# A decoder layer on one core: the last router scores and the second search move over the loop's edge, and the written order is renewed

## The reference

```
x = x + attention(norm(x))           # 16 heads of 32 columns, softmax over 224 keys, output product Wff
x = x + cross_attention(ctx, norm(x))# one head of 512 columns, softmax over 750 keys
x = x + ffn(norm(x)):
    query  = h @ q_proj.T ; rq = query @ router_w.T        # 48 columns
    scores = rq @ (aux_keys @ router_w.T).T / sqrt(48) + mask   # 224 x 2048
    top_scores, top_idx = top_k(scores, 8)
    agg  = sum over 8 of softmax(top_scores) * aux_values[top_idx]
    gate = sigmoid(w * clip(0.5 * log variance part + 2.5 * sigmoid(learned part)) + b)
    out  = h + gate * agg
```

## Time and profile before

| What | Value |
|---|---|
| median of the runs | 2769.6 us |
| the profiled execution: its time, its span | 2767.93 us, 2766.1 us |
| busy: PE, PEld, DVE, ACT, POOL | 2549.4, 2107.2, 1976.6, 1442.4, 862.9 us |
| PE busy between 400 and 2500 us | 2049.95 of 2100 us, granted clock 1.00 |
| one iteration, from A `score` 0 to the next | 79.1 us |
| DVE, ACT, POOL busy in one iteration | 60.9, 43.4, 26.0 us |
| PE busy between 2600 and 2700 us, and after 2700 us | 56.95 us, 0 us |
| DMA share between 2600 and 2766 us | 0.94 to 0.98 |

### The profile page before, as it was taken

The page is one execution under the profiler, slowest core; times in us unless marked ns, Lnnn a source line. Parts: engine busy times, 40 slices in busy tenths (PEclk is TensorE's granted clock), DMA queues, the critical chain, the costliest instruction groups (busy, mean ns, idle before and its releaser), DMA issues.

```text
span 2766.1 us, 55689 instructions
## 1 busy us (share of the span) xinstructions
PE 2549.4 (92%) x19090; PEld 2107.2 (76%) x19090; DVE 1976.6 (71%) x3087; ACT 1442.4 (52%) x4247; POOL 862.9 (31%) x811
## 2 busy tenths in 40 slices
PE   5999999999999999999999999999999999999840
PEld 3678878887888788878887888788878887888620
DVE  4445778877777787777777787777777877776552
ACT  2445555555555555555555555555555555555343
POOL 0001333323333333233333332333333323233344
PEclk9999999999999999999999999999999999999965
DMA  6233455554444555444445454444454554443799
GB/s 188 57 79 80 108 133 128 134 129 137 123 121 115 132 126 136 129 134 123 124 115 132 124 137 129 132 128 121 117 132 123 137 129 131 127 122 105 198 213 201
DMA packets 131545, 358.88 MB, mean 130 GB/s; under 512 B 21908, under 2 KB 26516, under 8 KB 123269
## 3 DMA queue, kind: packets, MB, share of 16 engines
q0 software_dynamic: 63520, 160.60, 25.0%
q1 hardware_dynamic: 63190, 192.16, 24.7%
q10 hardware_dynamic: 4784, 5.46, 0.6%
HBM read 316.38 MB, written 41.78 MB: 129 GB/s over the span
## 4 chain that ended last, share of the span: by engine, by line
PE 78%; DVE 8%; ACT 5%; issue 4%; DMA 2%; POOL 1%; ACTq 1%; DVEq 0%; POOLq 0%
PE psX L1150 41%; PE psA L1150 17%; PE psA L1159 6%; PE psF L1150 5%; PE psA L1216 4%; PE psA L1239 3%; PE psX L1159 2%; ACT L769 1%; DMA vg<-in_L_ffn_aux_values,idx 1%; DVE xmax L955 1%; PE psF L1159 1%; DVE top L1006 1%; ACT xT_hi L687 1%; DVE oT_lo L902 1%; DVE idx L1009 1%
## 5 line engine op out<-in xcount | busy, mean ns | idle before, releaser
L613 POOL DMA_INDIRECT vg<-in_L_ffn_aux_values,idx x512 | 542.8, 1060 | 1208.1 <-issue 1071.3
L708 ACT ACTIVATE pa<-psA,nmax 112x224 f32<-112x224 f32 x1024 | 443.6, 449 | 191.3 <-DVE nmax L924 184.5
L924 DVE TENSOR_REDUCE nmax<-psA 112x4 f32<-112x896 f32 x256 | 267.2, 1086 | 151.8 <-PE psA L1216 151.8
L1035 DVE SCALAR_TENSOR_TENSOR agg<-vg,wt,agg 112x512 f32<-112x512 f32 x406 | 361.6, 891 | 10.7
L1150 PE MATMUL psX<-big,gT 128*112 128x375 f32 x1024 | 333.4, 478 | 0.6 <-ACT gT L735 0.6
L1150 PE MATMUL psX<-pT,cx 125*128 125x224 f32 x1536 | 299.1, 355 | 0.0
L1150 PEld LDWEIGHTS psX<-pT,cx 125*128 125x128 f32 x1536 | 288.0, 190 | 4.0 <-issue 0.3
L939 DVE TENSOR_TENSOR pa<-pa,rsum 112x896 f32<-112x896 f32 x256 | 279.6, 1092 | 8.8
L1150 PEld LDWEIGHTS psX<-big,gT 128*112 128x112 f32 x1024 | 175.5, 176 | 125.7 <-issue 0.9
L1159 PE MATMUL psA<-ident,pa 112*112 112x112 f32 x2048 | 229.4, 263 | 24.9 <-DVE oT_lo L902 24.9
L1159 PEld LDWEIGHTS psA<-ident,pa 112*112 112x112 f32 x2048 | 202.0, 134 | 57.2 <-DVE oT_lo L902 31.5
(11 more groups left out here) (211 smaller groups left out, 5915.7 us busy)
## 6 DMA issues: line engine op xcount, KB each, us to landing
big<-in_ctx_t SPq DMA_DIRECT2D x32, 1500.0 KB, 6.3
cx<-in_ctx SPq DMA_DIRECT2D x32, 1344.0 KB
xa<-in_x SPq DMA_DIRECT2D x64, 224.0 KB, 2.9
centered<-in_x_t SPq DMA_DIRECT2D x32, 448.0 KB, 4.6
x<-in_L_attn_bff POOLq DMA_DIRECT2D x32, 448.0 KB
x<-cb_scratch POOLq DMA_DIRECT2D x32, 448.0 KB, 5.7
x<-in_x SPq DMA_DIRECT2D x31, 448.0 KB, 5.1
out<-x SPq DMA_DIRECT2D x30, 448.0 KB, 3.3
```

Of the source, the lines that this page charges most:

```text
L613: pool.indirect_dma_start(vg[:, c % SLOTS, k, :], None, aux_values, bass.IndirectOffsetOnAxis(ap=idx[:, t, n:n + 1], axis=0))\
L708: last = nc.scalar.activation(pa[:, t, h, :], psA[0:R, h, t * S:(t + 1) * S], ACT.Exp, bias=nmax[:, k % 2, h, t:t + 1], accum_out=rsum[:, ...
L924: nc.vector.tensor_reduce(nmax[:, k % 2, h:h + 2, :], psA[0:R, h:h + 2, 0:T * S].rearrange("p h (t s) -> p h t s", t=T), AX_X, ALU.max, ne ...
L1035: last = nc.vector.scalar_tensor_tensor(dst, vg[:, c % SLOTS, k, :], w, dst, ALU.mult, ALU.add)
```

## The change

`("F", "score", 3)` and `("F", "top", 1)` leave `ORDER`. Their work comes back as `("G", "score", 3)` and `("G", "top", 1)` near the start of the next iteration, with the same functions, for the same batch (stream G is one iteration behind F). The bank numbers of the jobs are kept: the job of `F score 3` is counted behind all of `ORDER`. At the same time the rest of `ORDER` stands in another sequence, and `LAST` opens with the two steps for batch 29. No instruction is added or removed in any batch.

Cut to its core:

```diff
 ORDER = (
-    ("A", "score", 0), ("N", "stat", 0), ("A", "share", 0), ("X", "enter", 0), ("X", "enter", 1), ("A", "qk", 2),
-    ("G", "gather", 1), ("N", "root", 0), ("X", "stat", 0), ("X", "root", 0), ("X", "norm", 0), ("A", "value", 0),
-    ("N", "spread", 0), ("X", "turn", 0), ("F", "stat", 0), ("G", "sum", 2), ("A", "prob", 0), ("F", "root", 0),
-    ("F", "norm", 0), ("X", "query", 0), ("G", "sum", 3), ("A", "score", 1), ("G", "gather", 2), ("F", "turn", 0),
-    ("A", "share", 1), ("X", "score", 0), ("A", "qk", 3), ("G", "sum", 4), ("X", "score", 1), ("N", "center", 0),
-    ("F", "route", 0), ("X", "prob", 0), ("A", "mix", 0), ("A", "prob", 1), ("F", "learn", 0), ("F", "score", 0),
-    ("G", "sum", 5), ("A", "mix", 1), ("X", "prob", 1), ("F", "score", 1), ("A", "score", 2), ("F", "top", 0),
-    ("G", "gather", 3), ("A", "share", 2), ("X", "mix", 0), ("X", "mix", 1), ("G", "sum", 6), ("A", "prob", 2),
-    ("F", "score", 2), ("A", "score", 3), ("G", "sum", 7), ("X", "out", 0), ("F", "score", 3), ("A", "share", 3),
-    ("X", "out", 1), ("A", "mix", 2), ("A", "prob", 3), ("F", "top", 1), ("F", "gather", 0), ("Q", "qk", 0),
-    ("R", "load", 0), ("F", "sum", 0), ("Q", "qk", 1), ("A", "mix", 3), ("R", "bias", 0), ("F", "sum", 1),
+    ("G", "score", 3), ("A", "score", 0), ("N", "stat", 0), ("X", "enter", 0), ("X", "enter", 1), ("X", "stat", 0),
+    ("A", "share", 0), ("A", "qk", 2), ("A", "value", 0), ("A", "prob", 0), ("G", "gather", 1), ("X", "root", 0),
+    ("X", "norm", 0), ("X", "turn", 0), ("G", "top", 1), ("A", "score", 1), ("N", "root", 0), ("F", "stat", 0),
+    ("F", "root", 0), ("X", "query", 0), ("F", "norm", 0), ("N", "spread", 0), ("G", "sum", 2), ("G", "sum", 3),
+    ("A", "share", 1), ("F", "turn", 0), ("X", "score", 0), ("A", "qk", 3), ("X", "score", 1), ("G", "gather", 2),
+    ("N", "center", 0), ("F", "route", 0), ("A", "mix", 0), ("X", "prob", 0), ("A", "prob", 1), ("F", "learn", 0),
+    ("F", "score", 0), ("G", "sum", 4), ("G", "sum", 5), ("X", "prob", 1), ("F", "score", 1), ("A", "score", 2),
+    ("G", "gather", 3), ("F", "score", 2), ("F", "top", 0), ("A", "share", 2), ("X", "mix", 0), ("X", "mix", 1),
+    ("A", "mix", 1), ("G", "sum", 6), ("A", "prob", 2), ("A", "score", 3), ("X", "out", 0), ("A", "share", 3),
+    ("X", "out", 1), ("R", "load", 0), ("A", "mix", 2), ("G", "sum", 7), ("A", "prob", 3), ("F", "gather", 0),
+    ("Q", "qk", 0), ("F", "sum", 0), ("Q", "qk", 1), ("A", "mix", 3), ("F", "sum", 1), ("R", "bias", 0),
 )
 LAST = (
-    ("G", "gather", 1, 29), ("Z", "load", 14, 31), ("X", "enter", 0, 31), ("X", "enter", 1, 31),
+    ("G", "gather", 1, 29), ("G", "score", 3, 29), ("G", "top", 1, 29), ("Z", "load", 14, 31), ("X", "enter", 0, 31),
...
-for _s, _step, _arg in (("A", "qk", 0), ("A", "qk", 1)) + ORDER:
+for _s, _step, _arg in (("A", "qk", 0), ("A", "qk", 1)) + ORDER + (("F", "score", 3),):
...
-                           ("F", "turn"): turn("F", "turn", xnfT), ("F", "route"): route, ("F", "score"): f_score,
-                           ("F", "top"): f_top})
+                           ("F", "turn"): turn("F", "turn", xnfT), ("F", "route"): route, ("F", "score"): f_score, ("G", "score"): f_score,
+                           ("F", "top"): f_top, ("G", "top"): f_top})
...
-                          ("F", "route"): route, ("F", "learn"): learn, ("F", "score"): f_scores})
+                          ("F", "route"): route, ("F", "learn"): learn, ("F", "score"): f_scores, ("G", "score"): f_scores})
```

More of the change, by code:

```diff
@@ L1140, in _ @@
                            ("X", "mix"): u_lo, ("X", "out"): x_out,
-                           ("F", "norm"): f_norm, ("F", "route"): route, ("F", "learn"): learn, ("F", "top"): f_top,
+                           ("F", "norm"): f_norm, ("F", "route"): route, ("F", "learn"): learn, ("F", "top"): f_top, ("G", "top"): f_top,
                            ("G", "sum"): g_sum, ("F", "sum"): g_sum})
```

## The result

The changed kernel takes 2782.04 us, the median of six runs (2778.3 to 2785.17). The kernel before took 2770.14 us in six runs beside them (2767.43 to 2773.61). The ratio is 1.0044, with a 95% interval of 1.0033 to 1.0055. The change makes the kernel 0.4% slower, which is 11.9 us, where 13.4 were predicted. The profiled execution is the slowest of the six, 2785.17 us with a span of 2783.4.

A forecast was written before the change was run, and what follows sets the result against it. PE bounds the loop, time changing only where it waits. The terms sum to +0.42 us an iteration, +12.2 over 29; with 1 for the tail, 2767.9 gives 2781, and the median 2783 us; 8 in 10 between 2763 and 2806.

The forecast's parts named there:

- the 1 us for the tail: In `LAST`, `top` 1 of batch 29 ahead of X `enter` on VectorE: 0 to 4.7 us, taken as 1.
- F `score` 3 in the gap, −0.91: As G `score` 3 it fits PE's wait before A `score` 0, gaining 0.91 us an iteration.
- that rival: Loop's edge delays G `score` 3: 2795 us at 0.5, 2812 at 1.1; chance 0.18 together with the store.
- A `prob` 1, −0.35: ScalarE no longer copies X `prob` 0 before `oT_hi`, so PE's wait falls by 0.35 to some 0.48 us.
- A `score` 3 and F `score` 2, +1.0: Without F `score` 2 between, PE waits about 1.0 us for A `prob` 2's copies before A `score` 3.
- A `score` 1 and X `query`, +0.31: A `score` 1 behind A `prob` 0 and X `turn` waits 0.27 us; with X `query`'s wait, 0.31.
- X `score` 0, +0.17: It needs `gT`'s second half; only F `turn` covers this now, so PE waits 0.17 us.
- X `score` 1, +0.20: `top` 1 on VectorE makes `xmax` 1.2 us later; PE waits 0.2 us, between 0 and 0.7.
- F `root` at 0.71 us: Takes 0.71 us, not 1.20, as no VectorE sum runs beside it; F `norm` then just in time for F `turn`.
- The store as a rival: F `sum` 0 waits for the sums' store, PE loses 0.9 us an iteration: 2809 us; chance 0.18 with the edge.
- The waits shown: PE's waits: A `score` 3 near 1.0 us, A `prob` 1 near 0.5, small at A `score` 1, X `query`, X `score` 0 and 1.

The follow-up runs named there:

- The kernel with the swap undone: The changed kernel with A `mix` 0 behind X `prob` 0 again, as before the change: 2796.73 us, ratio 1.0100.
- the first experiment: The changed kernel with F `score` 2 moved back between A `prob` 2 and A `score` 3: 2780.1 us, ratio 1.0041.

## Why the prediction came true

The time, the sign and the pace came out as forecast: 2782 us against 2783, 79.60 us an iteration against 79.5. That the time is right to 1 us is partly luck. In the table A `prob` 1 is 0.14 us better than forecast and the small rows 0.15, while four rows are 0.04 to 0.19 worse, and these cancel; the loop lost 0.50 us an iteration where +0.42 was the forecast, and the 1 us for the tail can't be seen in its scatter. By its steps:

- *F `score` 3 in the gap, −0.91.* Right to 0.01 us in the table; 0.94 by the kernel with the edge undone and G `sum` 7 in front, 0.89 by the one with the edge alone. The edge itself costs nothing, which the prediction had to assume: that rival is gone.
- *A `prob` 1, −0.35.* Right in mechanism, −0.49 in size. The kernel with the swap undone shows it.
- *A `score` 3 and F `score` 2, +1.0.* Right in size, +1.01. The step that named its cause was only half the cause: it said that F `score` 2 "is done before X `mix`" and costs its own time there. In truth that time covers VectorE's late copy of X `prob` 1. The kernel that gave only this cover back gained nothing, and the +1.0 is a cost only together with the place of G `sum` 5.
- *A `score` 1 and X `query`, +0.31; X `score` 0, +0.17.* Measured 0.62 together. The excess is 0.10 at A `score` 1, which starts 2.67 us after A `prob` 0 and not 2.57, and some 0.04 in the group of X `query`. There the prediction had a wait of 0.04 ahead of X `query`, none ahead of F `turn` and 0.17 ahead of X `score` 0; start to start, X `query` is 0.17 longer and F `turn` 0.09.
- *X `score` 1, +0.20.* The size was a little low (0.26, and 0.09 more behind its first matmul); the step that explains it failed. It said that `xmax` is late because `top` 1 takes VectorE 4.66 us more between the two maxima. In the kernel with the edge undone `top` 1 is not in this stretch, VectorE idles there for 5.11 us before A `score` 1's maxima, and X `score` 0 to X `score` 1 takes as long as in the changed kernel. VectorE's rows at A `score` 1's maxima in the changed kernel, then these maxima and `xmax` with the edge undone:

```profile
1417.34 1.09 DVE L924 TENSOR_REDUCE nmax<-psA 112x4 f32<-112x896 f32 x1 [0.45 <-PE psA L1216]
...
1375.31 1.09 DVE L924 TENSOR_REDUCE nmax<-psA 112x4 f32<-112x896 f32 x1 [5.11 <-PE psA L1216]
...
1388.68 0.93 DVE L955 TENSOR_REDUCE xmax<-psX 112x1 f32<-112x750 f32 x1
```

From A `score` 1's maxima to `xmax` VectorE takes 13.37 us in both (1417.34 to 1430.71, 1375.31 to 1388.68), with `top` 1 ahead or without it: `top` 1 fills time in which VectorE would wait for A `score` 1. So what makes `xmax` late is the chain that begins with A `score` 1's maxima and goes through F `stat`, F `root`, F `norm`, the sums and the `share`. Moving A `score` 1 back, with the sums, put `xmax` back at 30.34 us (30.32 before the change) with `top` 1 still there. Which of these instructions alone sets it was not tried.
- *F `root` at 0.71 us.* Right. All 32 are short now; the earlier trace rows had 1.20 in most. F `norm` was just in time, as forecast, but for some 0.08 us by which F `turn` started late:

```profile
L603 POOL TENSOR_TENSOR rstd_F<-ve_F,power x32: 688/689/724, 227.3 to 2664.4; 112x2 f32<-112x2 f32 x32
...
1423.28 5.08 DVE L1035 SCALAR_TENSOR_TENSOR agg<-vg,wt,agg 112x512 f32<-112x512 f32 x4
1423.44 2.80 POOL L592 TENSOR_TENSOR x<-x,nx 112x1024 f32<-112x1024 f32 x1 [1.22 <-DVE nx L869]
```

No sum of VectorE runs beside F `root` any more, and `add_base` still stretches the sums: four of them took 5.08 us, where a pair without it took 1.54 (the timeline of the first experiment). The Trainium skill, "SBUF — State Buffer", section "Who interferes with whom", has it as its rule that a VectorE instruction with two inputs in SBUF contends with a GpSimd one that reads SBUF. The traces agree with it, by 0.69 against 1.20 us.
- *The store as a rival.* Refuted: F `sum` 0 doesn't wait for it, and the signal had come within 3.9 us. The Trainium skill, "Perfetto Trace Analysis", section on the HWDGE DMA instruction, warns of a long delay of such signals; it cost nothing here.
- *The waits shown.* I had given them as sizes to be seen. 1.0 at A `score` 3 shows as 0.82, and 0.27 at A `score` 1 as 0.20. At X `query`, X `score` 0 and X `score` 1 none shows: X `query` does follow A `score` 1 without a wait (0.80 us, 0.81 before), but the steps from X `query` to X `score` 0 are 0.26 longer start to start, and those from X `score` 0 to X `score` 1 as well.

The tail's 1 us stays open: the part behind the last bias load takes 182.9 to 193.4 us in kernels that all end with the same `LAST`.

## What to carry to other kernels

In an order that all engines share, every step on PE covers several drains at once; before a step is moved, list each wait that it covers where it stands and where it goes, and give back covers in pairs. Follow each half of a moved step on its own engine: here the search's small half on ScalarE and one sum on VectorE cost 3.75 us an iteration (81.96 to 78.21, the falls of the clock included), the step itself 0.91. Judge a change by the pace and by start-to-start times of the steps, not by the waits that the profile shows.

## What was not expected of the hardware

- Shown waits are too small: 0.82 us shown is 1.06 start to start at A `score` 3, and 11.6 us fewer shown waits went with a slower kernel.
- TensorE's granted clock fell to 0.5 in some iterations once PE waited 2.0 or 2.28 us in one place (16 and 8 times between 400 and 2500 us); with 1.1 us there, none fell. A fall cost 1.5 us where it lasted 3.4 us, and 2.8 where it lasted 6.8. What decides in which iterations it falls is open.
